# The second layer norm's variance, power and Newton step moved from VectorE to GpSimd, and GpSimd's sums over two tiles at a time

## What is computed

```python
v = jnp.var(x); (x - m) / jnp.sqrt(v + eps)            # layer norm, per row of 64
H = gelu(xf @ W1 + b1)                                 # 64 -> 256
probs = softmax(H @ Wg + bg); assign = argmax(probs)   # 8 experts
out = sum over e of (assign == e) * probs[e] * (H @ Wd[e] + bd[e])
h = h + out
```

## Time and profile before

| | |
|---|---|
| median of 3 timed runs | 725.24 us (716.4, 725.36, 725.24) |
| the profiled execution | 716.47 us, of which the span of instructions is 714.3 us |
| busy: PE, DVE, ACT, POOL | 609.4, 546.8, 265.3, 385.2 us (85, 77, 37, 54%) |
| mean granted TensorE clock | 0.947 of full speed |

### The profile page before, as it was taken

One profiled execution on the slowest core, in us unless ns is written; L12 is line 12 of the kernel. 1 busy time (PEld: TensorE's weight loads), 2 busy tenths in 40 slices (PEclk: granted clock), 3 DMA queues, 4 the chain that ended last, 5 costly groups with the idle time before them and its releaser, 6 DMA issues. The chain is left out here.

```text
span 714.3 us, 9724 instructions
## 1 busy us (share of the span) xinstructions
PE 609.4 (85%) x3015; PEld 435.9 (61%) x3015; DVE 546.8 (77%) x1050; ACT 265.3 (37%) x689; POOL 385.2 (54%) x477
## 2 busy tenths in 40 slices
PE   0799899939957999999836988888988888899995
PEld 0477677736646878787623655556655555566563
DVE  7688888874976778888535888888888788888864
ACT  2222322226631222222346544555444455554310
POOL 1789999310540333333441566765676566657656
PEclk9999999988958999999956999999999999999998
DMA  6200000000000000000000000000000000000001
GB/s 239 46 1 0 0 1 1 0 0 1 0 1 0 1 0 1 0 0 1 0 0 1 2 15 16 16 15 0 16 16 16 16 16 16 16 0 16 15 16 29
DMA packets 13011, 9.75 MB, mean 14 GB/s; under 512 B 4396, under 2 KB 12716, under 8 KB 12716
## 3 DMA queue, kind: packets, MB, share of 16 engines
q1 hardware_dynamic: 12956, 9.28, 4.2%
q10 hardware_dynamic: 16, 0.00, 0.0%
HBM read 5.08 MB, written 4.20 MB: 13 GB/s over the span
## 5 line engine op out<-in xcount | busy, mean ns | idle before, releaser
L1372 PE MATMUL ex_pE<-ex_WdP,ex_hid 128*128 128x512 f32 x774 | 203.9, 406 | 0.0
L1372 PEld LDWEIGHTS ex_pE<-ex_WdP,ex_hid 128*128 128x128 f32 x774 | 139.6, 189 | 43.3 <-issue 8.1
L1673 POOL TENSOR_TENSOR ex_s<-ex_ms 128x1024 f32<-128x1024 f32 (+1 forms) x33 | 77.4, 2345 | 111.7 <-DVE ex_ms L1512 111.7
L1512 DVE TENSOR_TENSOR ex_ms<-ex_pE,ex_gate 128x512 f32<-128x512 f32 x129 | 88.4, 685 | 50.3 <-PE ex_pE L1372 49.9
L723 DVE TENSOR_TENSOR inv_prod<-inv_pW,m_img 128x504 f32<-128x504 f32 x144 | 91.6, 681 | 17.4 <-PE inv_pW L638 15.7
L1195 POOL TENSOR_TENSOR hT<-hT,ssm_gelu 128x512 f32<-128x512 f32 x32 | 47.7, 1509 | 95.8 <-ACT ssm_gelu L1168 95.8
L649 PE MATMUL inv_pS<-ident,inv_prod 128*128 128x128 f32 x576 | 87.8, 275 | 6.2 <-DVE inv_prod L723 5.5
L649 PEld LDWEIGHTS inv_pS<-ident,inv_prod 128*128 128x128 f32 x576 | 70.0, 141 | 28.7 <-DVE inv_prod L723 20.8
L638 PE MATMUL inv_pW<-inv_ysb,m_conv2L 98*128 98x512 f32 x144 | 69.4, 485 | 2.3 <-DVE inv_ysb L711 2.3
L1436 ACT ACTIVATE ex_hidf<-ex_pH,b1c 128x512 f32<-128x512 f32 (+1 forms) x68 | 45.2, 665 | 56.9 <-PE ex_pH L1325 56.9
L1341 PE MATMUL ex_pGR<-ex_hid,ex_WgP 128*32 128x512 f32 (+1 forms) x136 | 38.3, 430 | 28.8 <-DVE ex_res L1605 26.6
(11 more groups left out here) (239 smaller groups left out, 1061.9 us busy)
## 6 DMA issues: line engine op xcount, KB each, us to landing
m_img<-in_x SPq DMA_DIRECT2D x2, 2048.0 KB, 9.2
out<-ex_res SPq DMA_DIRECT2D x16, 256.0 KB, 2.3
WdT<-in_L_ffn_Wd SPq DMA_DIRECT2D x2, 256.0 KB
W1d<-in_L_ffn_W SPq DMA_DIRECT2D x2, 64.0 KB
bd<-in_L_ffn_bd SPq DMA_DIRECT2D x8, 2.0 KB
m_Bm<-in_L_attn_fwd_B_real SPq DMA_DIRECT2D x2, 16.0 KB, 2.0
m_Bm<-in_L_attn_fwd_B_imag SPq DMA_DIRECT2D x2, 16.0 KB, 2.0
m_Bm<-in_L_attn_bwd_B_real SPq DMA_DIRECT2D x2, 16.0 KB, 2.0
```

The costliest lines, as they stand in the source:

```text
L1372: last = nc.tensor.matmul(pE[n % 3][0:P].rearrange("p e f -> p (e f)"), hid[i % 2][value][:, h, par, 128 * j:128 * j + P], WdP[weight][:, ...
L1512: nc.vector.tensor_tensor(ms[b % 2][0:P, t % TILES, :].rearrange("p (e f) -> p e f", e=EX), pE[n % 3][0:P], gate[i % 2][0:P, t, :].unsquee ...
L1673: nc.gpsimd.tensor_tensor(s4[0:P, 0:T], m[:, :, 0:4 * F], m[:, :, 4 * F:], ALU.add).then_inc(halved, 1)
```

## The change

The scaling of the mean is dropped: `minus_sum` reduces with a negated sum, and `squares` scales the rows by 64 instead, so that the squares come out 64^2 too large and the variance is taken with 1/64^3. `variance`, `power` and Newton's four instructions become one function `factor` of six instructions on GpSimd, with buffers `fac` of their own by item parity; `normalise` on VectorE keeps only the wide multiply. `tree` sums two tiles at a time (`TPB`), four times an item (`NB`), from four buffers `ms`; GpSimd's order becomes `tree` over tiles 0 and 1, `tree` over 2 and 3, `factor(i+3)`, and two more `tree`. The diff (context lines as they are, "..." between its pieces):

```diff
...
     AHEAD = 4
     NH = 6
     TPI = 2 * TILES
+    TPB = 2
+    NB = TPI // TPB
     GATE = 11
     with ExitStack() as ctx:
         def sem(name):
...
 
         hs = [sb(f"hs{n}", [128, TPI, F]) for n in range(NH)]
         sq = sb("sq", [128, 2, TPI, F])
-        stat = [sb(f"stat{n}", [128, 4, TPI]) for n in range(2)]
+        stat = [sb(f"stat{n}", [128, 2, TPI]) for n in range(2)]
         half = sb("half", [128, TPI])
-        fac = sb("fac", [128, 3, TPI])
+        fac = [sb(f"fac{n}", [128, 4, TPI]) for n in range(2)]
         xn = sb("xn", [128, TPI, F])
         u = [[sb(f"u{n}{t}", [128, CH], F32R) for t in range(2)] for n in range(2)]
         hidf = sb("hidf", [128, 2, 2, CH])
...
         gate = [sb(f"gate{n}", [128, TPI, EX]) for n in range(2)]
         inverse = sb("inverse", [128, TPI, EX + 1])
         gs = sb("gs", [128, 4, TPI])
-        ms = [sb(f"ms{n}", [128, TILES, EX * F]) for n in range(2)]
-        s4 = sb("s4", [128, TILES, 4 * F])
-        s2 = sb("s2", [128, TILES, 2 * F])
-        s1 = sb("s1", [128, TILES, F])
+        ms = [sb(f"ms{n}", [128, TPB, EX * F]) for n in range(NB)]
+        s4 = sb("s4", [128, TPB, 4 * F])
+        s2 = sb("s2", [128, TPB, 2 * F])
+        s1 = sb("s1", [128, TPB, F])
         picked = [sb(f"picked{n}", [128, TPI, F]) for n in range(2)]
         res = [sb(f"res{n}", [128, TPI, F]) for n in range(2)]
 
         w1_made, w1_parted, wg_parted, wd_parted, wg_high = (sem(n) for n in ("w1_made", "w1_parted", "wg_parted", "wd_parted", "wg_high"))
         consts, filled = sem("consts"), sem("filled")
-        turned_in, rested, meaned, squared = sem("turned_in"), sem("rested"), sem("meaned"), sem("squared")
-        sums, varied, powered, newton, normed = sem("sums"), sem("varied"), sem("powered"), sem("newton"), sem("normed")
+        turned_in, rested, summed, squared = sem("turned_in"), sem("rested"), sem("summed"), sem("squared")
+        newton, factored, normed = sem("newton"), sem("factored"), sem("normed")
         turned_out, u_high, u_made = sem("turned_out"), sem("u_high"), sem("u_made")
         hidden, gelued, parted = sem("hidden"), sem("gelued"), sem("parted")
         judged, leveled, gated, tanhed, dv = sem("judged"), sem("leveled"), sem("gated"), sem("tanhed"), sem("dv")
...
             return 1 if is_cls(i) else TPI
 
         def batches(i):
-            return 1 if is_cls(i) else 2
+            return 1 if is_cls(i) else NB
 
         with nc.Block() as block:
             @block.tensor
...
                     nc.scalar.copy(u[i % 2][0][:, 0:cols(i)], pXU[:, 0:cols(i)]).then_inc(u_high, 1)
 
                 def squares(i):
-                    act.wait_ge(meaned, i + 1)
+                    act.wait_ge(summed, i + 1)
                     if i >= 2:
-                        act.wait_ge(varied, i - 1)
+                        act.wait_ge(factored, i - 1)
                     P = rows(i)
                     for t in range(groups(i)):
-                        last = nc.scalar.activation(sq[0:P, i % 2, t, :], hs[i % NH][0:P, t, :], ACT.Square, bias=stat[i % 2][0:P, 1, t:t + 1],
-                                                    accum_out=stat[i % 2][0:P, 2, t:t + 1])
+                        last = nc.scalar.activation(sq[0:P, i % 2, t, :], hs[i % NH][0:P, t, :], ACT.Square, scale=float(F),
+                                                    bias=stat[i % 2][0:P, 0, t:t + 1], accum_out=stat[i % 2][0:P, 1, t:t + 1])
                     last.then_inc(squared, 1)
 
                 def add_bg(i):
...
                 def rest(i):
                     act.wait_ge(turned_in, i + 1)
                     if i >= NH:
-                        act.wait_ge(reduced, 2 * (i - NH) + 2)
+                        act.wait_ge(reduced, NB * (i - NH + 1))
                     P, n = rows(i), 128 * columns(i)
                     nc.scalar.copy(hs[i % NH][0:P, 0:groups(i), :].rearrange("p t f -> p (t f)"), pXU[0:P, 0:n]).then_inc(rested, 1)
 
...
             def _(v):
                 def multiply(i, t):
                     n = TPI * i + t
-                    b = 2 * i + t // TILES
+                    b = NB * i + t // TPB
                     P = rows(i)
                     v.wait_ge(spoke, n + 1)
                     if t == 0:
                         v.wait_ge(dv, GATE * (i + 1))
-                    if t % TILES == 0 and b >= 2:
-                        v.wait_ge(halved, b - 1)
-                    nc.vector.tensor_tensor(ms[b % 2][0:P, t % TILES, :].rearrange("p (e f) -> p e f", e=EX), pE[n % 3][0:P],
+                    if t % TPB == 0 and b >= NB:
+                        v.wait_ge(halved, b - NB + 1)
+                    nc.vector.tensor_tensor(ms[b % NB][0:P, t % TPB, :].rearrange("p (e f) -> p e f", e=EX), pE[n % 3][0:P],
                                             gate[i % 2][0:P, t, :].unsqueeze(2).broadcast_to([P, EX, F]), ALU.mult).then_inc(chosen, 1)
 
                 def part(i, h, par):
...
                     nc.vector.tensor_tensor(hid[i % 2][1][:, h, par, c], hidf[:, h, par, c], hid[i % 2][0][:, h, par, c],
                                             ALU.subtract).then_inc(parted, 1)
 
-                def mean(i):
+                def minus_sum(i):
                     v.wait_ge(rested, i + 1)
                     P, T = rows(i), groups(i)
-                    st = stat[i % 2]
-                    nc.vector.tensor_reduce(st[0:P, 0, 0:T], hs[i % NH][0:P, 0:T, :], AX.X, ALU.add).then_inc(sums, 1)
-                    v.wait_ge(sums, i + 1)
-                    nc.vector.tensor_scalar(st[0:P, 1, 0:T], st[0:P, 0, 0:T], -1.0 / F, None, ALU.mult).then_inc(meaned, 1)
+                    if i >= 2:
+                        v.wait_ge(squared, i - 1)
+                    nc.vector.tensor_reduce(stat[i % 2][0:P, 0, 0:T], hs[i % NH][0:P, 0:T, :], AX.X, ALU.add,
+                                            negate=True).then_inc(summed, 1)
 
                 def low(i):
                     v.wait_ge(u_high, i + 1)
                     c = slice(0, cols(i))
                     nc.vector.tensor_tensor(u[i % 2][1][:, c], pXU[:, c], u[i % 2][0][:, c], ALU.subtract).then_inc(u_made, 1)
 
-                def variance(i):
-                    v.wait_ge(squared, i + 1)
-                    P, T = rows(i), groups(i)
-                    st = stat[i % 2]
-                    nc.vector.tensor_scalar(st[0:P, 3, 0:T], st[0:P, 2, 0:T], 1.0 / F, LN_EPS, ALU.mult, ALU.add).then_inc(varied, 1)
-
                 def normalise(i):
                     P, T = rows(i), groups(i)
-                    var = stat[i % 2][0:P, 3, 0:T]
-                    guess, corr, factor = (fac[0:P, n, 0:T] for n in range(3))
-                    v.wait_ge(powered, i + 1)
-                    nc.vector.tensor_tensor(corr, guess, guess, ALU.mult).then_inc(newton, 1)
-                    v.wait_ge(newton, 4 * i + 1)
-                    nc.vector.tensor_tensor(corr, corr, var, ALU.mult).then_inc(newton, 1)
-                    v.wait_ge(newton, 4 * i + 2)
-                    nc.vector.tensor_scalar(corr, corr, -0.5, 1.5, ALU.mult, ALU.add).then_inc(newton, 1)
-                    v.wait_ge(newton, 4 * i + 3)
-                    nc.vector.tensor_tensor(factor, guess, corr, ALU.mult).then_inc(newton, 1)
-                    v.wait_ge(newton, 4 * i + 4)
+                    v.wait_ge(factored, i + 1)
                     if i >= 1:
                         v.wait_ge(turned_out, i)
-                    nc.vector.tensor_tensor(xn[0:P, 0:T, :], hs[i % NH][0:P, 0:T, :], factor.unsqueeze(2).broadcast_to([P, T, F]),
+                    nc.vector.tensor_tensor(xn[0:P, 0:T, :], hs[i % NH][0:P, 0:T, :], fac[i % 2][0:P, 3, 0:T].unsqueeze(2).broadcast_to([P, T, F]),
                                             ALU.mult).then_inc(normed, 1)
 
                 def choose_best(i):
...
                                             ALU.mult).then_inc(dv, 1)
 
                 def finish(i):
-                    v.wait_ge(reduced, 2 * i + batches(i))
+                    v.wait_ge(reduced, NB * i + batches(i))
                     v.wait_ge(biased, i + 1)
                     if i >= 2:
                         v.wait_ge(stored[i % 2], 16 * (i // 2))
...
                     if more:
                         part(i + 1, 0, 1)
                     if there(i + 3):
-                        mean(i + 3)
+                        minus_sum(i + 3)
                     if now > 2:
                         multiply(i, 2)
                     if more:
...
                         low(i + 2)
                     if now > 5:
                         multiply(i, 5)
-                    if there(i + 3):
-                        variance(i + 3)
                     if more:
                         choose_best(i + 1)
                     if now > 6:
...
 
             @block.gpsimd
             def _(pool):
-                def power(i):
+                def factor(i):
+
```

(38 more changed lines are left out.)

## The result

The changed kernel takes 692.77 us in the median (692.19 to 695.23, four runs), against 721.88 for the kernel before (716.4 to 725.36). The ratio is 0.961, with a 95% interval of 0.953 to 0.969: 3.9% faster. The profiled execution took 692.19 us, its span is 690.0.

A forecast was written before the change was run, and what follows sets the result against it. VectorE's late `finish`, delayed by Newton's stalls, was taken to hold TensorE at `judge`. Gains 16.8 + 1.4 + 2.0 + 2.3 = 22.5 us off 716.47 gave 694, or 703 on the upper level; 699 was named, range 684 to 714.

The forecast's parts named there:

- (1): Last stage's windows: Newton's four small instructions and their stalls leave VectorE, 4.0 us a window on the path.
- (5): Start of the last stage: the scaling of the mean, held up by a GpSimd product, goes; net 1.4 us gained.
- (2): VectorE's chain up to `judge`: third multiply bound by `speak` 2 at t + 6.45; without collisions the 2 us wait vanishes.
- (3): Last stage's windows: GpSimd's sums collide with VectorE's subtractions, leaving `judge` a 0.7 us wait; 16.8 us gained.
- (4): GpSimd's load in a window: 16.2 us against 12.7 before, `factor` in time with three microseconds of room; costed at nothing.
- (6): End of the last stage: the final sum covers two tiles, 3.3 us, instead of four, 5.3 us; 2.0 us gained.
- (7): TensorE's clock falls in three windows, 1.55 us each; shorter waits spare half of it, 2.3 us gained.
- The 5 us on top: Whole kernel: timed runs stood on two levels 8.8 us apart; forecast 694 or 703, so 699 was named.
- (B): Rival, last stage: no collision matters, `judge`'s wait vanishes and the clock holds; 34.7 us less, 682 us; chance 0.18.
- (C): Rival, last stage: collisions eat most, `judge` still waits 1.6 of 2.0 us; 7.6 us less, 709 us; chance 0.21.
- (D): Rival, last stage: VectorE's five wide two-input instructions each wait for a whole sum; 30 us more, 747; chance 0.04.
- The estimate of 0.33 us: GpSimd's `factor`: a small product taking 0.33 us there would make it 0.7 us longer, inside its room.

The follow-up runs named there:

- e9: Changed kernel with four chained, unused 128x8 two-input products put on VectorE ahead of each xn from item 4 on: 699.86 us.
- e3: Kernel before with one move in VectorE's order, normalise(i+3) with Newton ahead of the window's last multiply: 697.92 us.
- e4: Changed kernel with six unused wide reductions put on VectorE before each xn from item 4 on: 746.83 us.
- e1: Changed kernel with sums set back to four tiles and two buffers, leaving only the factor moved to GpSimd: 690.76 us.
- e2: Kernel before with only the sums changed, two tiles at a time from four buffers, Newton still on VectorE: 710.86 us.
- e5: Changed kernel with four-tile sums from two buffers, except the last item's last four tiles, summed by two: 688.06 us.
- e6: Changed kernel with GpSimd's first sum of a window held until four tiles are multiplied instead of two: 691.98 us.
- e7: Changed kernel with two unused wide reductions (1.4 us) put on VectorE ahead of xn: 692.47 us.
- e8: Changed kernel with four unused wide reductions (2.8 us) put on VectorE ahead of xn: 703.41 us.
- e10: Changed kernel with four chained, unused small one-input reductions put on VectorE ahead of each xn from item 4 on: 690.01 us.

## Why the prediction was right

It named 699 us, 684 to 714, faster; measured 692.8. Step by step:

(1), the Newton stall on the path, 4.0 us a window: shown. e9 brings a stall back with products that compute nothing (1.5 us of it), e3 avoids it with the work left on VectorE, and e4 puts a hole as long as Newton's in the same place and gets windows of 20.7 us. The rule behind it was too narrow: it named instructions with both inputs in SBUF, while the scaling of the mean, which (5) itself reads as held up, has one; the scaling L1572 above shows the same.

(2), the chain after it: right. The third multiply starts at t + 6.5 (said 6.45).

(3), the new collisions: right in kind and place, mis-sized. The wait left is 0.3 us a window (4.7 in 14, with 0.7 in the first), not 0.7, so 21.9 us came instead of 16.8. About the middle of 0 and 1.2 us was taken for what the last two subtractions lose; they lose 0.34 (1.62 less 1.28). In the timeline the second halving starts at 582.70 and has 0.2 us left when the third subtraction is issued at 583.24, and what follows it on GpSimd is 128x128, 0.46 us, and partly waits itself. The worst case, a whole step of the sum ahead of each, doesn't come up in this window. That both engines are in step with the multiplies may be the reason; no run tests it.

(4), GpSimd's load: said 16.2 us, measured 16.3. The 128x8 forms take 0.20 us, the lower bound. `factor` ends at t + 15.8 and xn never waits for it in a full window.

(5), the start: said 1.4, measured 2.1 in a stretch in which the clock differed too (0.54 before, 0.56 after), so how much of it is the scaling of the mean stays open. (6), the end: said 2.0, measured 2.1.

(7), the clock: said half of the falls would stay away, all did. 25.9 us in the windows less 21.9 at `judge` leaves 4.0, for which 2.3 stood in the sum.

So the sum for the stage was 22.5, and 30.1 came. That the kernel's time is still near the sum (694) is luck: it is owed to the 5.8 us lost in stages that weren't touched. The 5 us on top, for the upper level of the runs, were wrong: the changed kernel's runs lie within 3 us, none near 703. (B), everything gained, was nearer for this stage (34.7) than the forecast. (C) and (D) fell: waits at `judge` of 1.6 us and more don't occur. The estimate of 0.33 us for GpSimd's small ones by the Trainium skill (GPSIMD Engine Reference, Performance versus the Vector engine) isn't borne out: 0.20.

What the prediction overlooked lies in the second part of the change: it costed the halved sums at the end of the kernel and as a new collision, but never asked what the windows would be without them. e1 shows 18.2.

## What to carry to other kernels

A small product on VectorE with both inputs in SBUF, or a small scaling there, takes up to as long as the GpSimd sum that it is issued behind (2.40 us in place of 0.17); a reduction doesn't. Look in the timeline for durations that are too long for their shape and end with a GpSimd instruction; then first try to move them in the order to where GpSimd idles (3.6% here, one move in the order), and then to GpSimd itself. When a part of a change is good at one place only, as short sums are at the end, do it only there.

## What the runs showed of the hardware that was not expected

TensorE's clock fell behind some of the longer waits, and that cost nearly as much as they did: in the kernel before 1.6 us of longer work in a window with a wait of 2.0; in the three windows of e4 with a clock of 0.86, 2.8 us (20.8 to 20.9 busy, against 18.05) with a wait of 3.0. In the kernel before, the stretch before and after one of the three slow `judge` (table by window):

```profile
556.00:560.00 4.00, 2.17 (x10) 1.43 (x8) 3.96 (x9) 3.16 (x17) 0.53 (x1) 1.00 0.00 0
560.00:564.00 4.00, 3.86 (x10) 2.06 (x11) 1.19 (x2) 0.50 (x1) 3.84 (x3) 0.57 0.22 66
564.00:568.00 4.00, 4.00 (x17) 2.23 (x15) 2.68 (x10) 0.43 (x2) 2.41 (x3) 1.00 0.00 0
```

TensorE was busy for 2.17 of 4 us, waiting at the end; in the next 4 us the granted clock was 0.57, so mostly its lower level of 1.2 GHz, then again 1.00. In the one profiled execution of each kernel, where `judge` waited 0 to 1.5 us on average, the clock held in all fourteen windows: the changed kernel, e1, e2, e3, e5, e6, e7, e8 and e10. In the kernel before twelve windows have a wait of 2.0 us, and three of them fell; in e4 twelve have 2.7 to 3.0 us, and seven of them fell. One window near the end of e9 fell as well, with a wait of 1.9 us. Which windows fall isn't settled: windows with the same wait did and didn't, and two in e2 with 2.0 and 2.1 us of idle time held.

The power on GpSimd, 1.65 us long, didn't exclude VectorE's two-input products: the earlier trace rows, and in e3 the same product took 0.23 us, issued 0.4 us into it:

```profile
573.84 1.65 POOL L1664 TENSOR_TENSOR ex_fac<-ex_stat,ex_half 128x8 f32<-128x8 f32 x1
...
574.24 0.23 DVE L1570 TENSOR_TENSOR ex_gl<-ex_gl,ex_gs 128x64 f32<-128x64 f32 x1
```

That it reads its operands early and then computes would explain it; no run tests that.
